# The weights of W and g move to the head of the load queues, and Z is computed ahead of batch 0's Gram products

## What is computed

```
g_x     = (g_w @ x_2 + g_b)^T            # 1024 x 256
theta_x = (theta_w @ x + theta_b)^T      # 1024 x 256
phi_x   =  phi_w @ x_2 + phi_b           # 256 x 1024
W  = theta_x @ phi_x / 1024              # 1024 x 1024
y  = (W @ g_x)^T                         # 256 x 1024
wy = w_w @ y + w_b
out = bn_gamma * (wy - bn_mean) * rsqrt(bn_var + 1e-5) + bn_beta + x
```

## Time and profile before

| | |
|---|---|
| median of 3 runs | 748.43 us (748.29 to 748.54) |
| profiled execution, its own time | 747.87 us |
| its span in the profile | 746.1 us |
| granted TensorE clock | 1.00 |
| busy: TensorE, VectorE, ScalarE, POOL | 99%, 78%, 66%, 45% |

### The profile page before, as it was taken

One profiled execution on the slowest core, in us unless ns is written; L12 is line 12 of the kernel. 1 busy time (PEld: TensorE's weight loads), 2 busy tenths in 40 slices (PEclk: granted clock), 3 DMA queues, 4 the chain that ended last, 5 costly groups with the idle time before them and its releaser, 6 DMA issues.

```text
span 746.1 us, 12821 instructions
## 1 busy us (share of the span) xinstructions
PE 739.7 (99%) x3795; PEld 636.5 (85%) x3795; DVE 583.8 (78%) x1296; ACT 489.6 (66%) x1341; POOL 334.6 (45%) x239
## 2 busy tenths in 40 slices
PE   8999999999999999999999999999999999999998
PEld 6688988889888888988889888888888889888886
DVE  3887878868787787878868787787887868788685
ACT  5666785757767576775766857576775766857341
POOL 5947252462706437162462615527163462615500
PEclk9999999999999999999999999999999999999999
DMA  9926556272744709366182754708366182650202
GB/s 261 229 83 124 228 119 236 51 210 93 179 173 88 260 5 238 112 113 239 41 221 89 150 201 79 247 25 230 122 113 239 30 214 108 132 221 11 117 1 114
DMA packets 92108, 107.18 MB, mean 144 GB/s; under 512 B 8602, under 2 KB 73012, under 8 KB 92084
## 3 DMA queue, kind: packets, MB, share of 16 engines
q1 hardware_dynamic: 88896, 105.83, 49.4%
q10 hardware_dynamic: 3188, 1.05, 0.7%
HBM read 73.28 MB, written 33.59 MB: 143 GB/s over the span
## 4 chain that ended last, share of the span: by engine, by line
PE 97%; ACT 1%; DVE 1%; ACTq 0%; issue 0%; POOL 0%; DVEq 0%
PE wbank L939 59%; PE gbank L939 37%; PE wbank L985 1%; ACT room L494 1%; ACTq L185 0%; PE wbank L963 0%; DVE mt L860 0%; PE wbank L991 0%; ACT ctxT_hi L471 0%; POOL ctxT_lo L397 0%; DVE stage L865 0%; PE wbank L975 0%; DVE q_lo L895 0%; DVE room L844 0%; PE wbank L1116 0%
## 5 line engine op out<-in xcount | busy, mean ns | idle before, releaser
L397 POOL TENSOR_TENSOR ctxT_lo<-ctxT,ctxT_hi 128x512 fp32r<-128x512 f32 x124 | 160.0, 1318 | 294.5 <-ACT ctxT_hi L471 294.5
L446 POOL TENSOR_TENSOR x_lo<-x_sb,x_hi 128x1024 fp32r<-128x1024 f32 x60 | 142.5, 2410 | 0.0
L929 DVE SCALAR_TENSOR_TENSOR x_sb<-wbank,const,x_sb 128x512 f32<-128x512 f32 x110 | 77.4, 746 | 70.5 <-PE wbank L939 70.5
L588 ACT ACTIVATE mt<-stage 32x224 fp32r<-32x224 f32 (+1 forms) x210 | 70.2, 334 | 94.6 <-DVE stage L727 90.1
L494 ACT ACTIVATE room<-ctx_sb 128x256 f32<-128x256 f32 x240 | 96.3, 403 | 19.5 <-issue 19.5
L939 PE MATMUL gbank<-ctxT_lo,ctxT_hi 128*128 128x512 f32 x360 | 84.0, 389 | 0.0
L939 PE MATMUL gbank<-z_hi,mt 128*128 128x512 f32 x256 | 81.7, 390 | 0.0
L939 PE MATMUL wbank<-x_hi,wt_hi 128*128 128x512 f32 x256 | 79.6, 392 | 0.0
L939 PEld LDWEIGHTS gbank<-ctxT_lo,ctxT_hi 128*128 128x128 f32 x360 | 67.6, 188 | 14.0
L681 DVE STREAM_TRANSPOSE ctxT<-ctx_sb 128x512 f32<-128x512 f32 x124 | 78.8, 682 | 0.7 <-DMA ctx_sb<-in_ctx_dram 0.7
L939 PE MATMUL wbank<-x_lo,wt_hi 128*128 128x512 f32 x256 | 79.0, 390 | 0.0
(11 more groups left out here) (150 smaller groups left out, 1526.3 us busy)
## 6 DMA issues: line engine op xcount, KB each, us to landing
out_dram<-x_sb SPq DMA_DIRECT2D x63, 512.0 KB, 4.6
ctx_sb<-in_ctx_dram SPq DMA_DIRECT2D x122, 256.0 KB, 4.6
x_sb<-in_x_dram SPq DMA_DIRECT2D x15, 2048.0 KB, 7.8
s_row<-s_dram SPq DMA_DIRECT2D x15, 256.0 KB, 3.5
x_sb<-in_x_dram SPq DMA_DIRECT2D x2, 1024.0 KB, 12.2
ctx_sb<-in_ctx_dram SPq DMA_DIRECT2D x4, 128.0 KB, 3.7
ctx_sb<-in_ctx_dram ACTq DMA_DIRECT2D x4, 128.0 KB, 4.0
ctx_sb<-in_ctx_dram ACTq DMA_DIRECT2D x2, 256.0 KB, 7.7
```

The source lines that it names most:

```text
L397: nc.gpsimd.tensor_tensor(ctxT_lo[:, c, :], turned_ctx(b, c), f(ctxT_hi[:, c, :]), ALU.subtract).then_inc(sem_, 1)
L446: nc.gpsimd.tensor_tensor(x_lo[:, k, :], x_sb[par][:, k, :], f(x_hi[:, k, :]), ALU.subtract).then_inc(x_lo_made, 1)
L588: return nc.scalar.activation(dst, src, ACT.Copy)
L929: nc.vector.scalar_tensor_tensor(out=x_sb[par][:, m, cols], in0=OUT_BANK[m][h][:, :], scalar=const[:, m:m + 1], in1=x_sb[par][:, m, cols], ...
```

## The change

The loads of w and g are split in halves, one half of each per queue, and stand ahead of the context. ScalarE issues all its pieces of the context behind its root. The warm-up is 9 products. ScalarE scales two quarters of w and VectorE the other two; TensorE turns w and makes Z before batch 0's first chunk; the two copies to wsT go to VectorE and ScalarE. High and low parts of Z are interleaved with the first four chunks on these two engines, and chunks 4 to 7 come behind the last z_lo. The first chunk's high*low products wait for the low parts of Z, whose banks they take over. The bias row ZB is made where w was turned. The bias vectors are turned behind chunk 3. The low part of x block 2 moves from POOL to VectorE; POOL makes that of block 3 between its fourth and fifth sum.

```diff
-    WARM_UP = 14
+    WARM_UP = 9
...
+        def load_w(eng, half):
+            ms = slice(half * (KC // 2), (half + 1) * (KC // 2))
+            eng.dma_start(w_nat[:, ms, :], w_w.rearrange("(m p) c -> p m c", p=P)[:, ms, :]).then_inc(in_w1, 16)
+        def load_g(eng, half):
+            eng.dma_start(g_nat[:, half, :], g_w.rearrange("(k p) c -> k p c", p=P)[half]).then_inc(in_w2, 16)
...
 # SP
+            load_w(sp, 0)
+            load_g(sp, 0)
             for piece in range(len(FIRST_PIECES)):
                 load_first_ctx(sp, (0, 1), piece)
             load_vectors(sp, range(0, 3))
-            sp.dma_start(w_nat, ...).then_inc(in_w1, 16)
+            load_first_x(0)
             sp.dma_start(theta_nat, ...).then_inc(in_w4, 16)
-            load_first_x(0)
             sp.dma_start(phi_nat[:, :, :], ...).then_inc(in_w3, 16)
-            sp.dma_start(g_nat, ...).then_inc(in_w2, 16)
             load_first_x(1)
...
 # POOL
             for c in range(CH):
+                if c == RING:
+                    pool.wait_ge(x_hi_made, KC)
+                    nc.gpsimd.tensor_tensor(x_lo[:, KC - 1, :], ...).then_inc(first_x_lo_pool, 1)
                 first_sum_up(c)
-            for k in (2, 3):
-                pool.wait_ge(x_hi_made, k + 1)
-                nc.gpsimd.tensor_tensor(x_lo[:, k, :], ...).then_inc(first_x_lo_pool, 1)
             first_sum_rest()
...
 # ScalarE
-            load_first_ctx(act, (2, 3), 0)
-            load_first_ctx(act, (2, 3), 1)
+            load_w(act, 1)
+            load_g(act, 1)
             act.wait_ge(ident_done, 2)
             nc.scalar.activation(tmp[:, 7, :], ident[:, 0:KC], ACT.Sqrt)
-            load_first_ctx(act, (2, 3), 2)
             act.wait_ge(vec_step, 1)
             nc.scalar.activation(tmp[:, 1, :], tmp[:, 0, :], ACT.Sqrt).then_inc(root_done, 1)
+            for piece in range(len(FIRST_PIECES)):
+                load_first_ctx(act, (2, 3), piece)
             load_vectors(act, range(3, 6))
-            hi(ident_r[:, :], ident[:, :], ident_r_made)
-            for c in range(CH):
-                ctx_hi(0, c)
             act.wait_ge(scale_made, 1)
-            act.wait_ge(in_w1, 16)
-            for m in range(KC):
+            act.wait_ge(in_w1, 16 * 2)
+            for m in (2, 3):
                 nc.scalar.activation(w_nat[:, m, :], w_nat[:, m, :], ACT.Identity, ...).then_inc(w_scaled, 1)
+            act.wait_ge(w_turned, 2)
+            hi(wsT[:, 1, :], W_BANK[1][:, :], w_taken_act)
+            hi(ident_r[:, :], ident[:, :], ident_r_made)
+            ctx_hi(0, 0)
+            z_hi_part(0)
+            ctx_hi(0, 1)
+            ctx_hi(0, 2)
+            z_hi_part(1)
+            ctx_hi(0, 3)
+            z_hi_part(2)
+            z_hi_part(3)
+            for c in range(RING, CH):
+                ctx_hi(0, c)
+            act.wait_ge(in_first_x[0], 16)
+            first_x_hi(0)
             act.wait_ge(ones_done, 1)
             act.wait_ge(vec_taken, 1)
...
 # VectorE
+            dve.wait_ge(scale_made, 1)
+            dve.wait_ge(in_w1, 16 * 2)
+            for m in (0, 1):
+                nc.vector.tensor_scalar(w_nat[:, m, :], w_nat[:, m, :], scale[:, m:m + 1], None,
+                                        ALU.mult).then_inc(w_scaled_dve, 1)
+            dve.wait_ge(w_turned, 2)
+            nc.vector.tensor_copy(wsT[:, 0, :], W_BANK[0][:, :]).then_inc(w_taken, 1)
+            dve.wait_ge(in_first[0], 16 * QT)
+            transpose_chunk(0, 0)
+            transpose_chunk(0, 1)
+            z_lo_part(0)
+            dve.wait_ge(in_first[1], 16 * QT)
+            transpose_chunk(0, 2)
+            transpose_chunk(0, 3)
+            for j in range(1, KC):
+                z_lo_part(j)
+            dve.wait_ge(in_first[2], 16 * QT)
+            for c in range(RING, CH):
+                transpose_chunk(0, c)
...
             first_x_lo_part(1)
+            first_x_lo_part(2)
+            dve.wait_ge(zb_done, 1)
+            nc.vector.tensor_copy(zb_row[:, :], ZB_BANK[:, :]).then_inc(zb_taken, 1)
...
 # TensorE
             for i in range(WARM_UP):
                 mm(wbank[0][:, :], ones_r[:, :], x_hi[:, 0, 0:HALF], True, True)
+            turn_w()
+            make_z()
...
                         for i in range(KC):
+                            if c == 0:
+                                pe.wait_ge(z_taken, (3, 3, 3, 4)[i])
                             ins = mm(FIRST_M_BANK[i][:, :], hi_of(c, i), ctxT_lo[:, c, :], c == 0, c == CH - 1)
...
-                    turn_w()
+                    make_zb()
                     turn_theta_phi()
```

More of the change, by code:

```diff
@@ L556, in z_hi_part @@
                 hi(z_hi[:, j, :], Z_BANK[j][:, :], z_hi_made)
+            ctx_hi(0, 0)
[8 more added lines that the diff above has]
+                ctx_hi(0, c)
             act.wait_ge(in_first_x[0], 16)
             first_x_hi(0)
+            act.wait_ge(ones_done, 1)
+            act.wait_ge(vec_taken, 1)
+            for k in range(KI):
+                nc.scalar.activation(bg_wide[:, k, :], f(ones_r[:, :]), ACT.Identity,
+                                     scale=bg_col[:, k:k + 1]).then_inc(wide_made, 1)
             first_x_hi(1)
+            act.wait_ge(in_first_x[1], 16)
+            first_x_hi(2)
+            first_x_hi(3)
             for i in range(KC):
@@ L987, in make_z, with make_zb @@
                     ins.then_inc(z_done, 1)
-                pe.wait_ge(tp_taken, 4)
+            def make_zb():
+                pe.wait_ge(vec_taken, 1)
                 pe.wait_ge(wide_made, KI)
@@ L1077, in theta @@
                                 pe.wait_ge(gram_f32, 3 * b + 3)
[L1078 removed]
+                        if m == 0 and first(b) and k < KC - 1:
                             pe.wait_ge(first_x_lo, k + 1)
                         elif m == 0 and first(b):
[L1081 removed]
+                            pe.wait_ge(first_x_lo_pool, 1)
                         elif m == 0:
```

81 lines of the change are left out of this document (22 added, 59 removed).

## The result

The changed kernel takes **757.21 us** (median of 4 runs, 756.89 to 758.12); the kernel before takes 748.36 us (747.99 to 748.54) beside it. The ratio is 1.0121, 95% interval 1.0109 to 1.0133: 8.9 us slower. The forecast was 751.1, its range 748.8 to 754.2. The direction is right, and the size is missed by 6.1 us. The profiled execution of the change is the longest of its four, 0.9 above the median; the forecast for the profiled one was 750.6, so there the miss is 7.5.

The account below looks back on a forecast made before the run. TensorE, busy 739.7 of 746.1 us, was taken to bound the kernel, a VectorE/ScalarE path ending within 0.2 us of it. TensorE +1.1, POOL's path +1.4, subtractions +0.2 made +2.7: 751.1 us, range 748.8 to 754.2.

Parts of the forecast that it names:

- Two such issues took 0.98, so six take 2.9 and end near 5.8 ... so ScalarE is free at 7.1: ScalarE's queue at the start: six context issues, then 1.3 us of vectors, before scaling w; turning then starts at 8.0.
- the dearer issues: ScalarE's queue: with a fuller queue an issue can cost up to 1.36 us; the range was said to include this.
- rival B: TensorE's clock falls while idle before Z: 1.65 us lost, 752.8, or 753.6 if turning is slow too; chance 18%.
- The loads: One MB of w and g ahead of the context: context landed below 18.7, cost nothing, up to 0.6 without cover.
- The Gram products: TensorE behind Z in batch 0: Z leaves at 16.7, Gram products end at 29.5, fourth low product waiting for z_lo(3).
- The wait for `tp_taken`: TensorE before theta(0): waits for VectorE's fourth subtraction, ending at 35.0, which puts theta and the T blocks +1.1 us.
- POOL's eight sums and one x_lo: POOL in batch 0: eight sums 12.0 us and one x_lo 2.35, after low parts of chunks 4 to 7 end at 24.6.
- The second path 1.4 beyond TensorE: POOL's sums, ScalarE's pack, th_lo, columns of s: +2.5 us, of which +1.1 is TensorE's own.
- rival A: POOL's path stays hidden and only TensorE's +1.1 us shows: 749.5; chance 20%.
- The subtractions beside POOL: Two VectorE subtractions ahead of the last t_hi meet POOL's low parts of batch 1: net -1.1 to +1.5, taken +0.2 us.
- x_lo on VectorE at nothing: VectorE takes one x_lo from POOL ahead of the bias row's copy, under TensorE's products: no cost, 2.35 us at most.
- Rival C: ScalarE's issues don't hold up its scalings, so w is turned 1.1 us earlier: 749.8, no change; chance 10%.

Follow-up runs that it names:

- Run 5: The changed kernel with SP issuing all four parts of the context's last piece, so ScalarE issues four pieces and not six: 754.01 us, ratio 1.0074.
- Run 2: The changed kernel with VectorE scaling all four quarters of w and making both copies to wsT: 752.72 us, ratio 1.0058.
- run 1: The changed kernel with 31 warm-up products and not 9: 754.45 us, ratio 1.0079.
- run 6: Run 5 with 17 warm-up products and not 9, filling TensorE's idle time ahead of the turning of w: 751.58 us, ratio 1.0042.
- run 7: The changed kernel with POOL summing chunks 0 to 3 ahead of its low parts of chunks 4 to 7: 755.85 us, ratio 1.0096.
- run 8: The changed kernel with the low part of x block 3 on VectorE too, so POOL makes none: 756.74 us, ratio 1.0115.
- run 4: The kernel before with w and g in halves heading both queues, ScalarE's context issues in their old order around its first activations: 752.69 us, ratio 1.0056.
- run 3: The kernel before with only the change's load order, ScalarE's six context pieces all behind its root: 754.95 us, ratio 1.0087.
- Run 11: Run 10 with ScalarE's pack moved behind the high parts of theta in batch 0: 748.31 us, ratio 1.0004.
- run 9: The changed kernel with the edits of runs 2, 5 and 7, weaker waits before theta(0) and Z, 10 warm-up products: 747.94 us, ratio 0.9994.
- Run 10: Run 9 with POOL summing two chunks early and not four: 748.06 us, ratio 0.9995.

## Why the prediction was wrong in size

**The step that failed first: "Two such issues took 0.98, so six take 2.9 and end near 5.8 ... so ScalarE is free at 7.1".** ScalarE was free at 10.5. The first two issues cost what the row said, 0.47 each, and the next four 1.25 each, the fifth 2.71 and the sixth 1.03; the six end at 8.86, 3.1 late, and the vectors add 0.3. Those 0.98 were the price of the same two pieces, the fifth and the sixth, in the kernel before, where no w and g stand ahead of them on the queue. The text did give the other end, 1.36 an issue, and the four later ones came near it; but it took the low value as nearest because it was ACT's own, and never carried the high one through the sum: six at 1.36 are 8.2, 5.3 later, which puts an end of the range at 756.4, though the stated range, to 754.2, says that it takes in "the dearer issues". Run 5 shows that the issues hold ScalarE: two fewer, scalings 3.2 sooner. Why an issue grows dear is not shown. Run 2 shows that nothing but ScalarE held the turning: the scale was there at 5.38 and w had landed.

**The second: the chance of rival B.** The low clock was given 18% and 1.65 to 2.5 us. It came, as a consequence of the first error: the forecast had TensorE idle for 1.5 us before the turning, and it was idle for 4.7. Against the forecast's terms the turning lost 1.0 and Z 2.6, 3.6 together; against run 1, where Z takes 6.54 and not 6.92, it is 0.9 and 3.0. Run 1 gives 3.2 of them back in the place of the first output product, with the turning 0.7 later, and run 6 gives back 2.4 us against run 5. Rival and forecast were priced as alternatives, though the late turning made the fall more likely: two errors that bring each other about don't belong in separate branches. And in run 5, whose turning at 8.27 is nearly the forecast's, it fell all the same, at about 10.2; in runs 7 and 8, where no transpose stood in the idle stretch, it fell at about 10.2 and 10.7, and in the change at 10.0. So the eight transposes of run 5 did not keep the clock. The Trainium skill (TensorE: Matmul & The Clock Gate, Part 4: PE-mode transpose) has transposes not counting as busy for the full clock; the prediction cited this and set it against transposes that stood between products. Run 5 is in line with the page, but it does not prove it: in run 4 the clock fell at about 12.6 although four true products had run from 11.04 to 11.86. No run put products in the place of the transposes. The trace of before never tested it.

**The loads: "Priced at nothing".** Wrong, but in the changed kernel itself hidden: chunk 4 waits for no DMA there. With Z on time (run 2) VectorE waits 1.75 for it, and the first output product is 2.1 further from Z's end than in run 6, more than three times the 0.6 given as the cost of lost cover. So with the issues at the forecast's price this term would have been the largest miss, at 752.7 still inside the range. The bound on which it rested, 18.7, did not hold in run 3 (20.35): it charged the added MB per byte, but ScalarE's last piece of context was also issued later, in the change at 5.09 and 7.83 and not from 3.39 on the earlier trace rows, and run 4 shows that this place is about half of it.

**The Gram products.** 13.3 from Z's end to the bias row, against 12.8. The first chunk's fourth low product waits for z_lo(3), which ends at 25.70, 1.9 behind Z's end and not 1.36. Together that is +0.5.

**What held.** From the bias row on, the differences to the forecast are nearly constant: theta(0) 42.61 against 35.0 (+7.6), T blocks 48.87 against 41.2 (+7.7), POOL's end 52.3 against 44.3 (+8.0), first output product 67.45 against 59.9 (+7.6). And 4.46 (Z's start, 14.26 against 9.8), 2.6 (its length) and 0.5 (Gram) make 7.6. Of the 4.46, 3.46 is the start of the turning, 11.46 against 8.0, and 1.0 the slow turning. By its terms:
- The wait for `tp_taken`: 0.7 forecast ahead of theta, 0.83 measured. Right.
- POOL's eight sums and one x_lo: 14.3 forecast, 33.04 to 47.6 measured, 14.5. The three last steps took 3.9 and not 4.7, the four low parts 6.03 and not 5.05. Right as a sum.
- The second path 1.4 beyond TensorE: run 7, which takes only that away, is 1.5 shorter behind Z, and rival A is refuted for this kernel.
- The subtractions beside POOL: net +0.2 forecast, and by luck near. In the chain of after the two are 0.74 and 1.04, against 1.53 and 0.33 in the chain of before; net -0.1. By the rule of the Trainium skill (SBUF — State Buffer, Who interferes with whom) each of two could lose a POOL step. Both did run beside POOL's low parts, and against the 0.41 of a subtraction that meets none they lost some 0.3 and 0.7, a part of a step (about 1.3) each, where before one lost 1.1. Run 11 shows that the sum depends on phase.
- x_lo on VectorE at nothing: right. VectorE waited 0.66 for TensorE behind it. One more block there was not free (run 8).
- Rival C, that issues don't hold up ScalarE's scalings: refuted by the 6.59 and 3.41 us of idle time put down to issue.
- The forecast's sign of failure, "if transposed chunk 4 waits for a DMA", did not come; Z's length, over 8 us, was the sign named for B, and it did. No sign was named for a Z that starts late, which is what happened.

Run 6 checks the sum behind Z as a whole: from Z's end to the first output product 43.67 against the forecast's 43.2 (16.7 to 59.9), and with full clock and Z's end 0.7 late the kernel takes 751.58. The chances for "same" and "faster" add up to 29 and 6 in the text and to 30 and 5 by its rivals, which changes nothing.

What stays open: runs 9 to 11 have the whole change, mended, and tie with before. Run 10 spends 0.7 less on TensorE up to the T blocks and loses it on the path to q_lo. Whether an order exists in which both are short wasn't tried further. Why the issues grow dear just at the fifth and sixth of context on ScalarE's queue was not taken apart by number and by size.

## What to carry to other kernels

An instruction queue that issues DMAs and also computes must have its computing ahead of the issues, or the issues elsewhere: the price of an issue read where less stands ahead of it on the queue did not hold with two large loads more (0.49 became 2.71 and 1.03). When work is moved to the start of a kernel, see what TensorE does until then, and keep products running right up to it; eight transposes between two idle stretches did not keep the clock here. Carry every bound that you write down through the sum to a time, and ask whether two rivals have a common cause.

## What the runs showed of the hardware

- In the changed kernel issuing a DMA from ScalarE's queue took 0.47 us each for the first two of context and up to 2.71 for a later one with several issued ahead; SP's six of context took 4.96 in the changed kernel and 2.99 in the one before. A first small vector issued behind them took 0.90 in the changed kernel and 2.11 in run 9, the next ones 0.27.
- In the change the granted clock fell to 0.50 at about 10.0, in a TensorE idle from 6.8 to 11.46, and was back at about 20.3. In run 5 it fell at about 10.2, after products had ended at 6.8 and only eight transposes stood between 8.27 and 9.37; in run 3 at about 10.6, in an idle from 8.2 to 11.75; in run 4 at about 12.6, after an idle of 3.44 and with products running again from 11.04. With the transposes at 6.62 to 8.20 and Z from 9.67 it stayed 1.00 (run 2).
- At 0.50 eight transposes took 1.97 instead of the 1.03 of runs 1 and 6, and Z, two thirds of it at 0.50, 9.52 instead of 6.54.
- The column of the granted clock reads 1.00 from the first product in every trace, while the first warm-up products start 0.44 apart, and the eight transposes of run 2, right behind them, took 1.58 at a reading of 1.00.
- Moving POOL's work by 1 us against VectorE changed one subtraction from 0.73 to 1.50 us (runs 10 and 11).
